# A new order of the prologue, and of convolution, turn and dense matmuls where a dense tap begins

## The reference

```python
off1 = make_offset(conv3x3(x, tm1_w, tm1_b), conv3x3(x, tr1_w, tr1_b))
out = relu(batchnorm(deform_conv(x, off1, dcn1_w), bn1_g, bn1_b))
off2 = make_offset(conv3x3(out, tm2_w, tm2_b), conv3x3(out, tr2_w, tr2_b))
out = batchnorm(deform_conv(out, off2, dcn2_w), bn2_g, bn2_b)
y = relu(out + x)
q, k, v = wq @ y + bq, wk @ y + bk, wv @ y + bv     # per image, over 1024 pixels
scores = q.T @ k                                    # 1024 x 1024
return gamma * (v @ softmax(scores, axis=1)) + y
```

## Time and profile before

| | |
|---|---|
| three runs | 785.04, 787.93 and 788.89 us, median 787.93 |
| the profiled execution | 789.25 us, its span 787.4 us |
| TensorE matmul busy | 718.4 us, 91% of the span |
| VectorE busy | 590.4 us, 75% |
| ScalarE busy | 514.4 us, 65% |
| GpSimd busy | 462.3 us, 59% |
| gathers of layer 1 | from 17.45 to 313.88 us |
| gathers of layer 2 | from 337.78 to 633.73 us |

### The profile page before, as it was taken

The page is one execution under the profiler, slowest core; times in us unless marked ns, Lnnn a source line. Parts: engine busy times, 40 slices in busy tenths (PEclk is TensorE's granted clock), DMA queues, the critical chain, the costliest instruction groups (busy, mean ns, idle before and its releaser), DMA issues.

```text
span 787.4 us, 12252 instructions
## 1 busy us (share of the span) xinstructions
PE 718.4 (91%) x3379; PEld 439.9 (56%) x3379; DVE 590.4 (75%) x1605; ACT 514.4 (65%) x1285; POOL 462.3 (59%) x466
## 2 busy tenths in 40 slices
PE   7689999999889899949899999989898997899997
PEld 5455656555445445535466555545554542577786
DVE  4398879898778859469867999778775968677542
ACT  1387677787777767338776877777776755665332
POOL 3677777777777777067777777777777730000000
PEclk8589999999999999968999999999999999899999
DMA  5957866677777777176786676666777710000001
GB/s 185 309 166 233 258 196 200 200 209 201 205 203 205 206 210 196 52 214 179 236 264 201 198 203 200 195 204 204 202 204 210 203 53 0 1 1 28 1 27 55
DMA packets 55743, 132.22 MB, mean 168 GB/s; under 512 B 8399, under 2 KB 25072, under 8 KB 55676
## 3 DMA queue, kind: packets, MB, share of 16 engines
q0 software_dynamic: 35840, 117.47, 50.7%
q1 hardware_dynamic: 19820, 13.94, 5.6%
q10 hardware_dynamic: 16, 0.03, 0.0%
HBM read 120.86 MB, written 10.55 MB: 167 GB/s over the span
## 4 chain that ended last, share of the span: by engine, by line
PE 68%; DVE 11%; DMA 7%; ACT 6%; issue 5%; POOL 2%; DVEq 0%; SPq 0%; POOLq 0%; ACTq 0%
PE pair L1300 22%; PE pair L1313 9%; DMA G<-table,rowi 7%; PE bank L1439 5%; PE bank L1251 4%; PE bank L1253 4%; PE pair L1305 3%; PE pair L1286 3%; DVE V L892 2%; DVE U L892 2%; DVE nmax L1032 2%; POOL G L502 2%; PE bank L1120 2%; PE pair L1159 2%; PE pair L1421 2%
## 5 line engine op out<-in xcount | busy, mean ns | idle before, releaser
L502 POOL DMA_INDIRECT G<-table,rowi x448 | 454.4, 1014 | 174.2 <-issue 90.2
L1300 PE MATMUL pair<-ST,XT 128*128 128x512 f32 x512 | 246.5, 611 | 21.9 <-ACT CTD L629 21.9
L592 ACT ACTIVATE V<-G,wgt 128x128 f32<-128x128 f32 x448 | 178.8, 399 | 57.7 <-DMA G<-table,rowi 56.8
L594 ACT ACTIVATE U<-G,wgt 128x128 f32<-128x128 f32 x448 | 174.9, 390 | 0.0
L892 DVE SCALAR_TENSOR_TENSOR V<-G,wgt,V 128x128 f32<-128x128 f32 x448 | 155.4, 347 | 10.8 <-ACT U L594 10.8
L1300 PEld LDWEIGHTS pair<-ST,XT 128*128 128x128 f32 x512 | 98.1, 194 | 116.2 <-issue 69.6
L892 DVE SCALAR_TENSOR_TENSOR U<-G,wgt,U 128x128 f32<-128x128 f32 x448 | 155.8, 348 | 0.0
L942 DVE TENSOR_TENSOR ST<-pair,stacks 128x512 f32<-128x512 f32 x170 | 112.5, 684 | 54.1 <-PE pair L1286 53.0
L1313 PE MATMUL pair<-CT,dcn_T 128*128 128x512 f32 x224 | 115.4, 598 | 0.0
L651 ACT COPY CT<-bank 128x512 f32<-128x512 f32 x112 | 65.3, 583 | 57.5 <-PE bank L1253 45.1
L1251 PE MATMUL bank<-band,V 128*128 128x128 f32 x448 | 100.9, 276 | 0.6 <-ACT CT L651 0.6
(11 more groups left out here) (166 smaller groups left out, 734.7 us busy)
## 6 DMA issues: line engine op xcount, KB each, us to landing
table<-XT SPq DMA_DIRECT2D x16, 512.0 KB, 5.3
G<-table,rowi POOLq DMA_INDIRECT x448, 3.7
out_dram<-G SPq DMA_DIRECT2D x8, 256.0 KB, 2.0
X<-in_x_dram SPq DMA_DIRECT2D x3, 512.0 KB, 6.9
A<-in_L_conv_dcn_w_dram SPq DMA_DIRECT2D x2, 576.0 KB, 7.9
X<-in_x_dram SPq DMA_DIRECT2D x2, 256.0 KB, 2.9
table<-zeros SPq DMA_DIRECT2D x4, 16.0 KB, 2.0
qkv_nat<-in_L_conv_wv_dram SPq DMA_DIRECT2D x1, 64.0 KB
```

Of the source, the lines that this page charges most:

```text
L502: pool.indirect_dma_start(G[:, i % UNITS, r, :], None, table(n).rearrange("r (e k) -> r e k", e=2), bass.IndirectOffsetOnAxis(rowi[:, at:a ...
L592: act.activation(V[:, i % V_RING, r, :], G[:, i % UNITS, r, 0:C], ACT.Copy, scale=wgt[:, tile:tile + 1, 0])
L594: act.activation(U[:, i % V_RING, r, :], G[:, i % UNITS, r, 3 * C:4 * C], ACT.Copy, scale=wgt[:, tile:tile + 1, 3]).then_inc(scaled[l], 1)
L1300: pe.matmul(dense_acc, XT[:, g // IGROUPS * TS + t, :], ST[:, all_y % ST_RING, :], start=(t == 0), stop=(t == QT - 1)).then_inc(dense_mm[l ...
```

## The change

In both layers, ScalarE and VectorE get the hats and the scaling and corner sums of step 0 ahead of parts of image 1. VectorE computes the positions and rows of image 1 after the hats of group 1. In layer 1 the three `setup` calls move from before the hats to between their turns. TensorE turns both halves of the hats and step 0 before it spreads the first rows. In the steps i > 0 in which the first used row block begins a dense tap (`tap_starts`: step 3 of group 0, and then twice per group, 15 steps in a layer), TensorE does `conv(i - 1)`, `conv_dense` and `turn(i + 1)` before the row blocks instead of after them. The warm-up at the end of each layer has 4 matmuls instead of 6.

```diff
@@ -269,6 +269,7 @@
             return XN[l][:, n * HW + t * P:n * HW + (t + 1) * P]
 
         AHEAD = 2
+        assert AHEAD == 2
         TURN_AT = {n: 2 + 2 * (n - AHEAD) for n in range(AHEAD, N)}
         SUMS_AT = {n: TURN_AT[N - 1] + 2 + 3 * (n - AHEAD) for n in range(AHEAD, N)}
         TURN_FIRST = {at: n for n, at in TURN_AT.items()}
@@ -573,14 +574,6 @@
                 xt_copy(0)
                 z_copy(0)
                 u_copy(0)
-                for n in range(1, AHEAD):
-                    relu_input(n)
-                    xt_copy(n)
-                    z_copy(n)
-                    u_copy(n)
-                if l == 0:
-                    for i in range(1, 4):
-                        setup(i)
 
                 def scale(i, rows):
 
@@ -634,13 +627,23 @@
                         act.wait_ge(acc_stats[l], GROUPS)
                     act.copy(A[l][:, g * BANK:(g + 1) * BANK], conv_acc).then_inc(acc_cp[l], 1)
 
+                relu_input(1)
+                xt_copy(1)
                 hats_top(0)
+                z_copy(1)
                 hats_middle(0)
-                hats_copy(0, 0)
-                column_copy(0, 0)
+                u_copy(1)
                 act.wait_ge(wgt_ready, l * N + 1)
                 scale(0, range(GTILES))
+                hats_copy(0, 0)
+                if l == 0:
+                    setup(1)
+                column_copy(0, 0)
+                if l == 0:
+                    setup(2)
                 hats_copy(0, 1)
+                if l == 0:
+                    setup(3)
                 column_copy(0, 1)
                 scale(1, range(GTILES))
                 scale(2, range(GTILES))
@@ -874,13 +877,7 @@
                 positions(0, 1)
                 sample_rows(0, 1)
                 bilinear_weights(0)
-                for n in range(1, AHEAD):
-                    xt_copy(n)
-                    offsets(n)
-                dve.wait_ge(off_ready, l * N + AHEAD)
-                positions(1, AHEAD)
-                sample_rows(1, AHEAD)
-                dve.wait_ge(wgt_ready, l * N + 1)
+                xt_copy(1)
 
                 def corner_sums(i):
 
@@ -949,12 +946,17 @@
                 hats_first(0)
                 hats_split(0)
                 hats_last(0)
+                dve.wait_ge(wgt_ready, l * N + 1)
                 corner_sums(0)
+                offsets(1)
                 for now in USED[0]:
                     product(*now)
                 corner_sums(1)
                 add_halves(1)
                 hats_first(1)
+                dve.wait_ge(off_ready, l * N + AHEAD)
+                positions(1, AHEAD)
+                sample_rows(1, AHEAD)
                 for i, (g, s) in enumerate(BLOCKS):
                     more = i + 2 < NB
                     for now in USED.get(i + 1, ()):
@@ -1317,20 +1316,28 @@
                     pe.wait_ge(sel_ready, 1)
                 pe.wait_ge(identb_ready, 1)
                 turn_hats(0, 0)
+                if l == 0:
+                    setup(1)
                 spread_columns(0, 0)
                 if l == 0:
-                    pe.wait_ge(setup_cp, 4)
+                    setup(2)
+                turn_hats(0, 1)
+                if l == 0:
+                    setup(3)
+                spread_columns(0, 1)
+                turn(0)
                 pe.wait_ge(xt_dve, l * N + AHEAD)
                 pe.wait_ge(xt_act, l * N + AHEAD)
                 for now in USED[0]:
                     spread_rows(*now)
-                turn_hats(0, 1)
-                spread_columns(0, 1)
-                turn(0)
                 for now in USED[1]:
                     spread_rows(*now)
+                if l == 0:
+                    pe.wait_ge(setup_cp, 4)
                 for i, (g, s) in enumerate(BLOCKS):
-                    for now in USED.get(i, ()):
+                    rows = USED.get(i, [])
+                    tap_starts = i > 0 and rows and rows[0][1] % QT == 0
+                    for now in rows if not tap_starts else ():
                         use_dense(*now)
                     if i:
                         conv(i - 1)
@@ -1338,6 +1345,8 @@
                         conv_dense(*TAP_DONE[i - 1])
                     if i + 1 < NB:
                         turn(i + 1)
+                    for now in rows if tap_starts else ():
+                        use_dense(*now)
                     if i in TURN_FIRST:
                         image_in(TURN_FIRST[i])
                         turn_input(TURN_FIRST[i], 0)
@@ -1358,7 +1367,7 @@
                     for now in USED.get(i + 2, ()):
                         spread_rows(*now)
                 conv(NB - 1)
-                warm_up(6)
+                warm_up(4)
 
             pe.wait_ge(turned_cp[1], NB)
             pe.wait_ge(acc_cp[1], GROUPS)
```

## The result

The kernel after takes 783.46 us (median, 780.09 to 785.12, 11 runs), the kernel before 789.51 us beside it (785.04 to 791.78, 11 runs). The ratio is 0.9917, 95% interval 0.9902 to 0.9932: 0.8% faster, about 6.5 us. The forecast was 781, range 775 to 787.5. As a figure the forecast is 2.5 us too low; before itself took 1.6 us more beside after than in the three runs that the forecast was made from (787.93). Against those it said -6.9; the measured ratio gives -6.5.

What follows compares the result with a forecast made beforehand. GpSimd's gather stream was taken to bound the layers, TensorE following; 2.4 + 0.85 + 0.3 + 1.2 + 0.8 + 1.5 = 7.05 us off the median 787.93 gave 781, range 775 to 787.5.

Steps and rivals of the forecast that it cites:

- The gathers pace, TensorE follows: In both layers GpSimd's gather issue sets the time, 224 times 1.25 or 280 us per layer; TensorE follows with a lag.
- (c): Within a layer, TensorE matters if its lag grows until a ring slot is not free in time for a gather.
- Start of layer 1, -2.4: At gather 17 of layer 1, the 2.40 us wait for step 0's corner sums goes, since they start near 25.6.
- Warm-ups behind layer 1, -0.85: Four warm-ups at layer 1's end bring layer 2's first gather 0.85 us earlier, bounds 0 and 1.7.
- Warm-ups behind layer 2, -0.3: After layer 2, four warm-ups let the first projection start 0.3 us earlier, bounds 0 and -0.5.
- Start of layer 2, sums of step 2 about 0.9 later, worth 0: In layer 2's prologue, step 2's sums come at about 364 instead of 363.13; no slot is late at first.
- Rival B: Layer 2's gather stream runs dry near step 16, margin 1.38 us before: 783, counted within the main case's 0.58.
- Dense taps, -1.2 and -0.8: At tap starts conv(i-1) runs in the CTD wait, shortening the layers' tails: -1.2 us in layer 1, -0.8 in layer 2.
- Held gathers, -1.5: In both layers, shifted positions change which gathers last over 0.946 us: -1.5 us, between 0 and -8, some new ones +3.
- Rival A: Only the fixed parts count; layer tails and held gathers stay as they are: 784.4 us, chance 0.27.
- Rivals C: Slower: dense rows stand behind a turn that waits for VectorE's corner sums; 804 us at full price, chance 0.05.
- D: Much faster: the catch-up loses its four holds and the tails all their lag; 771.6 us, chance 0.10.

Runs made afterwards that it cites:

- e5: The kernel before with 448 of the 512 dense matmuls working on 128 of their 512 columns; 798.92 us, ratio 1.0121 to before.
- e1: The kernel before with only the new prologue order on ScalarE, VectorE and TensorE, both layers; 783.99 us, ratio 0.9958 to before.
- e9: The kernel after with the hats' first instruction and absolute value on one SBUF input each (wrong hats, grid left out); 777.41 us, ratio 0.9855 to before.
- e2: The kernel before with only the new order in steps where a dense tap starts; 786.16 us, ratio 0.9973 to before.
- e3: The kernel before with only four warm-ups instead of six at the end of each layer; 787.34 us, ratio 0.9981 to before.
- e6: The kernel after with the prologue order of before in layer 2 only; 781.05 us, ratio 0.9908 to before.
- e12: The kernel after with layer 2's old prologue order, run a second time, beside the unchanged kernel after; 782.50 us, ratio 0.9936 to before.
- e11: The kernel after, unchanged, profiled and timed once more; 780.28 us, ratio 0.9898 to before.
- e4: The kernel after with six warm-ups again instead of four; 783.98 us, ratio 0.9935 to before.
- e7: The kernel after with four warm-ups behind layer 1 and six behind layer 2; 782.75 us, ratio 0.9923 to before.

## Why the prediction was right, by its steps

- **The gathers pace, TensorE follows.** Shown by e5, and by GpSimd's own timeline, where the gaps are 0.30 us almost throughout. The exception is the one that the prediction listed as (c): in the first third of layer 1 TensorE's lag can make gathers wait. It does in the profiles with full dense rows that start early, and once in e1.
- **Start of layer 1, -2.4.** Right, and for the reason given. The sums of step 0 began at 26.72 (25.6 was said), those of steps 1 and 2 at 35.48 and 43.19, 2 us earlier than worked out. The term that was too large is the 1.8 for the weight set-ups: 35.48 is what the sum gives without it. The 2 for positions and rows was right (7.7 us from the sums of step 1 to those of step 2, where it had been 5.9). Over the profiles the last gather of layer 1 starts on average at 309.2 with the new prologue (the nine besides e9) and at 312.0 with the old one (before, e2, e3): -2.8.
- **Warm-ups behind layer 1, -0.85.** Measured -0.87, and a lower clock in two of nine profiles, +1.5 each: about -0.5 on average. Whether the clock is the warm-ups' price is open.
- **Warm-ups behind layer 2, -0.3.** The mechanism was right (0.36 at the projection), the sum was not: +0.84 in the profile of after, 0 to +0.3 in the best cases. The step that failed is the one that put a lower clock at nothing, since "TensorE would idle under 2 us there, and it idles longer in the prologues anyway". The attention has its own idle stretch of 2.8 us, behind which the clock does fall in some executions, and it costs 0.5 to 1.2 us there. That happens with six warm-ups too, so the loss is not shown to be theirs.
- **Start of layer 2, sums of step 2 about 0.9 later, worth 0.** 1.25 later; e6, e12 and e11 put its worth within 0.4% of nothing. Rival B did not come in layer 2 in any profile; the place where the stream runs into its slots is layer 1. The prediction read its margins as larger than they were: a gather that waits starts 0.75 us after the sum's end (gather 17 of before did), so the 1.38 at step 16 of layer 2 was 0.63 from a wait.
- **Dense taps, -1.2 and -0.8.** In layer 1 the way from the last gather to the statistics is 8.5 to 9.0 in the nine profiles with the whole new order (after, e2, e4, e6 to e9, e11, e12), 10.2 to 11.5 in before, e1 and e3: means 8.7 and 10.7, so -1.9. In layer 2 it is 8.4 to 9.0 and 9.0 to 9.2: -0.5. After's own 8.97 was the worst of these. The two terms are mis-sized in opposite senses and sum to -2.4 where -2.0 was said; e2's time says -2.1.
- **Held gathers, -1.5.** Measured -1.3 and -0.6 in the pair of profiles, but which places are hit is the execution's matter more than the change's. The profiles with the old prologue have held gathers in the same places, all but 305 to 319, which are hit only in kernels with the whole change or most of it. The streams of layer 2, here up to the start of the last gather, take 290.5 to 295.1 us in twelve profiles of both orders, and before's 295.0 was nearly the worst. What the gathers of the two layers lose to 0.946 us is 28.1 us on average in the three profiles with the old prologue and 26.3 in the nine with the new, 27.4 and 26.9 as medians, and after and e11, one kernel, differ by 4.4. So whether the change is worth anything in this term is not shown. The test "fewer than four gathers over 2.5 us" came true (one), but says little: e11, the same kernel, has three, and before four. That the sum came out within half a microsecond owes something to this, to the larger gain at the end of layer 1 and to the loss in the attention, which cancel.

Rival A (784.4) is nearer to the median of after (783.46) than the forecast is, but only since both were reckoned from 787.93. As a difference A said -3.55, the forecast -7.05, and -6.5 was measured, and A's idea, that the ends of the layers stay as they are, fell with the 1.9 us of layer 1. With the holds left out and the ends counted the sum is 5.55, 1 us from what was measured; the interval of the ratio (-5.4 to -7.7 us) holds both this and 7.05, so the times can't tell them apart. Rivals C and D did not come.

## What to carry to other kernels

Before pricing a change of order, find the engine whose instructions follow each other at a fixed pace with only their issue time between them; here it was the one that is 59% busy. Then price an edit only at the ends of that stream and at places where its waits exceed the issue time, and check for the catch-up after a prologue, where the busiest engine's lag can still reach it. Read two profiles of one kernel before a difference of 1 to 3 us in one stretch is put down to an edit, and look at the granted clock behind a warm-up that is taken out in several profiles: here it fell in some and not in others, with either number of warm-ups.

## What the hardware did that was not expected

- With three quarters of seven in eight dense rows left out, the kernel was 1.2% slower: TensorE's granted clock fell from 0.950 to 0.882 of full speed, and gathers lasted longer by 5.6 and 1.6 us in the two layers.
- A gather that lasts 0.946 us alone took up to 2.95 us across eight or nine VectorE instructions in a row, also across such with one SBUF input, and another execution of the same kernel held other gathers.
- The first gather goes at 16.1 to 16.4 us or at 17.2 to 17.5, with either prologue, and this goes with where TensorE's clock falls in the first 18 us: from about 15 in e2, e5, e7, e11 and e12, from 12.4 to 14.2 in the others. Two windows of 12 to 18 us, of after and of e11, with granted clocks of 0.63 and 0.74:

```profile
12.00:18.00 6.00, 2.47 (x16) 2.10 (x15) 3.38 (x19) 0.28 (x1) 0.47 (x1) 0.63 0.98 302
```

```profile
12.00:18.00 6.00, 2.40 (x15) 2.28 (x16) 4.51 (x25) 0.00 (x0) 1.53 (x2) 0.74 1.00 317
```
